# Step rows and input rows of a selective scan's unit, fetched by two transfers on two queues

## The chip, the cores and the metric

One Trainium2 chip, one of its cores. Its engines run their own instruction streams and meet at semaphores: PE (TensorE, with PEld for its weight loads), DVE (VectorE), ACT (ScalarE), POOL (GpSimd) and SP (SyncE, which here only issues transfers). An instruction that waits for a semaphore holds up everything behind it on its engine. 16 DMA engines carry out the transfers. The metric is device time of one launch in microseconds; lower is better.

## The reference

Two layers on x of (4 images, 16 x 16 pixels, 192 channels). The first is a gated state-space block: group norm, in-projection to 2 x 96 channels, a 3x3 depthwise convolution with silu, a selective scan in four directions, layer norm, gate, out-projection. The second is a linear attention (12 heads, 64 features) and then an attention in which 6 of the 12 heads are chosen for each image; both with layer norm and residual. The scan is the part that matters here:

```python
def step(h, inp):
    u_t, d_t, B_t, C_t = inp
    dA = jnp.exp(d_t[..., None] * As)
    h = h * dA + (d_t * u_t)[..., None] * B_t[:, :, None, :]
    y = jnp.einsum('bkcn,bkn->bkc', h, C_t)
    return (h, y)
```

with 96 channels, 16 states, 256 pixels, 4 directions and 4 images.

## The kernel before

Each engine's program is written out by hand. The work of the scan is cut into 96 units, numbered u. There are 8 scans (4 images x 2 pairs of directions), each of 12 units; a unit holds 16 channels x 8 states on the 128 partitions and 2 directions x 256 pixels along the row (512 elements). For a unit

- ScalarE makes the decay, exp(step x A), in two instructions (`expo`, L763),
- VectorE makes the drive, input x B (`drive_of`, L1055), and runs the scan itself (`scan`, L1066), in this order,
- GpSimd multiplies the states by C (`weigh`, L586),
- TensorE sums the 8 states of a channel, for three units at a time (`sum_states`, L1395 and L1401).

Decay and drive need the step sizes and the inputs (step x value) of 16 channels, each repeated on 8 partitions. For each scan these rows are made once, on 96 partitions (`step2`); the inputs' half is made by GpSimd (`pre_inp`, L575). SyncE writes them to DRAM (`keep_step`, L451, semaphore step_kept; two buffers in turn), and then reads them back for each unit with every row repeated 8 times (`repeat_step`, L463): one transfer of 512 KB, 128 rows of 4 KB, of which the first half is the steps and the second half the inputs. The tile `in_rep` has four slots; unit u + 4 goes where unit u was, so its transfer waits for decay u and drive u. The rows of C travel the same way, 256 KB at a time in rows of 2 KB (`repeat_c`, L444).

Between the units each engine does other steps of the two layers. Tables say after which unit: ACT_SIDE, DVE_SIDE, PE_SIDE, POOL_SIDE, SP_SIDE. "81: t1.0 gT.2 hT.1" in ScalarE's table means that after decay 81 it copies the turned probabilities of the odd heads of image 0 (three copies, L648), the gate of image 2 (L648) and the hidden state of image 1 (L838). TensorE's results go through four PSUM banks, `ring0` to `ring3`, in a fixed order: a bank is filled again only when the engine that reads it has said so (semaphores s_free0 to s_free3). A fixed number of filler matmuls (`fill_in`, L1235), whose results nobody reads, stands ahead of many of TensorE's steps.

The three loops around the change, in the units' order: SyncE does its side items of unit u and then fetches unit u + 4; ScalarE makes decay u and then its side items; VectorE makes drive u, scan u and then its side items.

Of the kernel before, what the change touches and what calls it, by code (L numbers as in the profile page):

```python
# [29 lines left out]
TOK = WAYS * L  # L30
# [3 lines left out]
SN = 8  # L34
GRP = P // SN
GROUPS = DI // GRP
PARTS = NS // SN
UNITS = PARTS * GROUPS
# [10 lines left out]
IN_SLOTS = 4  # L49
# [17 lines left out]
SLOT_COUNT = SCANS * UNITS  # L67
# [115 lines left out]
def hybrid_kernel(nc, x, in_proj_w, conv_w, conv_b, x_proj_w, dt_w, dt_b, A_logs, Ds, norm_g, norm_b, out_proj_w,  # L183
# [5 lines left out]
    with ExitStack() as ctx:  # L189
        ctx.enter_context(nc.allow_non_contiguous_dma(reason="small parameter vectors"))  # L190

        def sb(name, shape, dt=F32):
            return ctx.enter_context(nc.sbuf_tensor(name, shape, dt))
# [24 lines left out]
        def sem(name):  # L218
            return ctx.enter_context(nc.semaphore(name))


        step_rows = nc.dram_tensor("step_rows", [2, DI, 2 * TOK], F32, kind="Internal").ap()
# [7 lines left out]
        def bank(name):  # L230
            return banks[ring[name][1]]
# [58 lines left out]
        in_rep = sb("in_rep", [P, IN_SLOTS, 2, TOK])  # L290
# [57 lines left out]
        S["outd"] = [sem(f"s_outd{b}") for b in range(IMG)]  # L348
        S["x"] = [sem(f"s_x{n}") for n in range(IMAGES)]
        S["c_there"] = [sem(f"s_c_there{i}") for i in range(PARTS)]  # L350
        S["in_there"] = [sem(f"s_in_there{i}") for i in range(IN_SLOTS)]
        free = [sem(f"s_free{i}") for i in range(FINAL_RING)]
        pe_side, act_side, dve_side, pool_side, sp_side = (beside(s) for s in (PE_SIDE, ACT_SIDE, DVE_SIDE, POOL_SIDE, SP_SIDE))
# [5 lines left out]
        def reuse(eng, name):  # L359

            _, at, held = ring[name]
            if held:
                eng.wait_ge(free[at], held)
            elif at >= RING + PARTS + 1:
                eng.wait_ge(S["y_ev"], IMAGES)
            elif at >= RING:
                eng.wait_ge(S["state"], SLOT_COUNT)
# [23 lines left out]
        def unit(u):  # L391

            n, g = u // UNITS, u % UNITS
            third, q = g % GROUPS % CHUNKS, g % GROUPS // CHUNKS
            return n // PER_IMAGE, n % PER_IMAGE, g // GROUPS, PER_CHUNK * third + q
# [5 lines left out]
        def _(sp):  # L401
# [5 lines left out]
            for i in range(PARTS):  # L407
                rows = DIRS * GROUPS
# [25 lines left out]
            def keep_c(n):  # L434

                taken(sp, f"d{n}")
                sp.dma_start(c_rows[n % 2].rearrange("i s t -> (i s) t"), step2[DI:, 0, :]).then_inc(S["c_kept"], 16)

            def repeat_c(n, i):

                sp.wait_ge(S["c_kept"], 16 * (n + 1))
                if n:
                    sp.wait_ge(S["outp"], UNITS * (n - 1) + GROUPS * (i + 1))
                sp.dma_start(c_rep[:, i, :], c_rows[n % 2, i].unsqueeze(0).to_broadcast([GRP, SN, TOK])).then_inc(S["c_there"][i], 16)  # L444

            def keep_step(n):

                sp.wait_ge(S["step"], n + 1)
                if n >= 2:
                    sp.wait_ge(S["decay"], UNITS * (n - 1))  # L450
                sp.dma_start(step_rows[n % 2], step2[0:DI, :, :].rearrange("p a t -> p (a t)")).then_inc(S["step_kept"], 16)  # L451

            def repeat_step(u):

                _, _, _, g = unit(u)
                n = u // UNITS
                if u % UNITS == 0:
                    sp.wait_ge(S["step_kept"], 16 * (n + 1))
                if u >= IN_SLOTS:
                    sp.wait_ge(S["decay"], u - IN_SLOTS + 1)  # L460
                    sp.wait_ge(S["drive"], u - IN_SLOTS + 1)
                rows = step_rows[n % 2, GRP * g:GRP * (g + 1), :]
                sp.dma_start(in_rep[:, u % IN_SLOTS, :, :].rearrange("p a t -> p (a t)"),  # L463
                             rows.unsqueeze(1).to_broadcast([GRP, SN, 2 * TOK])).then_inc(S["in_there"][u % IN_SLOTS], 16)

            keep_c(0)
            keep_step(0)
            for u in range(2):
                repeat_step(u)
            for i in range(PARTS):  # L470
                repeat_c(0, i)
            for u in range(2, IN_SLOTS):
                repeat_step(u)
            def side(step, n):

                if step == "kc":
                    keep_c(n)
                elif step == "ks":
                    keep_step(n)
                else:  # L480
                    repeat_c(n, int(step[1]))

            for item in sp_side[0]:
                side(*item)
            for u in range(SLOT_COUNT):
                for item in sp_side[u + 1]:
                    side(*item)
                if u + IN_SLOTS < SLOT_COUNT:
                    repeat_step(u + IN_SLOTS)
# [9 lines left out]
        def _(pool):  # L499
# [78 lines left out]
            def weigh(u):  # L578

                _, _, part, c16 = unit(u)  # L580
                if u % GROUPS == 0:
                    pool.wait_ge(S["c_there"][part], 16 * (u // UNITS + 1))
                pool.wait_ge(S["state"], u + 1)
                if u >= SLOTS:
                    pool.wait_ge(S["y_mm"], u - SLOTS + 1)
                g.tensor_tensor(outp[:, u % SLOTS, :], state[:, u % STATE_SLOTS, :], c_rep[:, part, :],  # L586
                                ALU.mult).then_inc(S["outp"], 1)
# [53 lines left out]
        def _(act):  # L641
            a = nc.scalar

            def evac(name, *copies):

                fetched(act, name)
                for dst, src in copies:
                    ins = a.copy(dst, src)  # L648
                ins.then_inc(freed(name), 1)
# [103 lines left out]
            def expo(u):  # L753

                _, back, part, c16 = unit(u)
                slot = u % IN_SLOTS
                act.wait_ge(S["in_there"][slot], 16 * (u // IN_SLOTS + 1))
                if u >= DECAY_SLOTS:
                    act.wait_ge(S["state"], u - DECAY_SLOTS + 1)
                kept = slice(0, L - 1) if back else slice(1, L)  # L760
                for e in range(WAYS):
                    at = (part * DIRS + WAYS * back + e) * GROUPS + c16
                    ins = a.activation(decay[:, back, u % DECAY_SLOTS, e, kept],  # L763
                                       in_rep[:, slot, 0, :].rearrange("p (e l) -> p e l", e=WAYS)[:, e, kept],
                                       ACT.Exp, scale=a_neg[:, at:at + 1])
                ins.then_inc(S["decay"], 1)

            def turned_probs(n, j):

                if n:  # L770
                    act.wait_ge(S["weighed"], n)
                name = f"pt{n}{j}"
                evac(name, (probT[:, j % 2, j // 2, :], bank(name)[:, :]))
# [126 lines left out]
                side(*item)  # L900
            for u in range(SLOT_COUNT):
                expo(u)
                for item in act_side[u + 1]:
                    side(*item)
            for item in act_side[SLOT_COUNT + 1]:
# [4 lines left out]
        def _(dve):  # L910
# [135 lines left out]
            def drive_of(u):  # L1046

                _, _, part, c16 = unit(u)
                slot = u % IN_SLOTS
                if u % GROUPS == 0:  # L1050
                    dve.wait_ge(S["b_there"], PARTS * (u // UNITS) + part + 1)
                dve.wait_ge(S["in_there"][slot], 16 * (u // IN_SLOTS + 1))
                if u:
                    dve.wait_ge(S["state"], u)
                v.tensor_tensor(drv[:, :], in_rep[:, slot, 1, :], b_bc[part][:, :], ALU.mult).then_inc(S["drive"], 1)  # L1055
# [154 lines left out]
            for u in range(SLOT_COUNT):  # L1210
                drive_of(u)
                scan(u)
                for item in dve_side[u + 1]:
                    side(*item)
# [455 lines left out]
```

## Time and profile before

| | |
|---|---|
| runs (us) | 397.46, 397.60, 617.52; median 397.6 |
| the profiled execution | 396.75, of which the span of the core's instructions is 395.0 |
| mean granted TensorE clock | 0.988 of full |
| busy | PE 371.8 (94%), DVE 285.2 (72%), ACT 212.7 (54%), POOL 192.4 (49%) |
| moved by DMA | 61.85 MB, mean 157 GB/s over the span |
| in_rep transfers | 96 of 512 KB, median 6.5 us from issue to landing |

The run of 617.52 us stands apart from the other two. The units' scans start between 43 and 295 us of the span. Before that stand the norms, the weights and the first scan's rows; after it the end of the second layer for images 2 and 3. A busy PE counts fillers too.

### The profile page before, as it was taken

What the parts mean: (1) busy time and instruction counts of PE and PEld (TensorE: products, weight loads), DVE (VectorE), ACT (ScalarE), POOL (GpSimd) and SP (SyncE); (2) the same over time, 40 slices, a digit from 0 to 9 for tenths busy, and PEclk for the clock granted to TensorE, in tenths of its full rate; (3) what the DMA queues carried; (4) which work ended last, traced back from release to release, by engine and by line L of the source; (5) the groups of instructions that cost most, each with busy time, mean ns of one, the idle gap of its engine ahead of it and who ended that gap; (6) DMA issues with size and microseconds to landing.
All of it is one profiled execution on the core that took longest, in us unless ns stands there. A gap on an engine that the chain in (4) does not pass through costs nothing.

```text
span 395.0 us, 7870 instructions
## 1 busy us (share of the span) xinstructions
PE 371.8 (94%) x2805; PEld 288.6 (73%) x2805; DVE 285.2 (72%) x477; ACT 212.7 (54%) x553; POOL 192.4 (49%) x236
## 2 busy tenths in 40 slices
PE   7998969999999999999999999999999999999990
PEld 5878847787797775777767877767586668888770
DVE  4734887999689898999979989799793500553464
ACT  2576447567445574744855657836754431257530
POOL 5222673788187676579665725854362400210021
PEclk9999998999999999999999999999999999999996
DMA  5703999999979999988988996369910000000010
GB/s 115 138 19 100 239 263 254 255 284 262 232 176 256 243 241 264 248 212 223 252 189 222 248 240 171 92 189 253 246 49 1 2 0 2 0 22 2 1 42 20
DMA packets 26240, 61.85 MB, mean 157 GB/s; under 512 B 6935, under 2 KB 10969, under 8 KB 26201
## 3 DMA queue, kind: packets, MB, share of 16 engines
q1 hardware_dynamic: 26201, 61.35, 62.6%
q8 instruction: 22, 0.36, 0.4%
q14 instruction: 17, 0.14, 0.1%
HBM read 57.15 MB, written 4.19 MB: 155 GB/s over the span
## 4 chain that ended last, share of the span: by engine, by line
PE 77%; DVE 9%; DMA 5%; ACT 4%; issue 2%; POOL 1%; SPq 1%; POOLq 0%; ACTq 0%; DVEq 0%
PE ring L1235 15%; PE y_acc L1401 6%; PE ring L1524 5%; PE y_acc L1235 5%; PE ring L1518 5%; DMA in_rep<-step_rows 4%; DVE state L1066 3%; PE b_bc L1376 3%; PE y_acc L1395 3%; PE ring L1445 2%; PE ring L1469 2%; PE ring L1598 2%; PE ring L1535 2%; PE ring L1415 2%; PE ring L1428 2%
## 5 line engine op out<-in xcount | busy, mean ns | idle before, releaser
L586 POOL TENSOR_TENSOR outp<-state,c_rep 128x512 f32<-128x512 f32 x96 | 123.4, 1301 | 62.5 <-PE y_acc L1401 30.2
L1066 DVE TENSOR_TENSOR_SCAN state<-decay,drv 128x512 f32<-128x512 f32 x96 | 117.2, 1220 | 13.6 <-ACT decay L763 6.4
L763 ACT ACTIVATE decay<-in_rep,a_neg 128x255 f32<-128x255 f32 x192 | 86.1, 500 | 54.3 <-DMA in_rep<-step_rows 45.7
L1235 PEld LDWEIGHTS ring<-ident 128*128 128x128 f32 x726 | 90.8, 193 | 23.5 <-issue 15.9
L1235 PE MATMUL ring<-ident 128*128 128x128 f32 (+1 forms) x726 | 99.2, 281 | 4.1 <-ACT room_h L678 2.9
L1055 DVE TENSOR_TENSOR drv<-in_rep,b_bc 128x512 f32<-128x512 f32 x96 | 66.4, 692 | 10.7 <-PE b_bc L1376 2.0
L601 POOL TENSOR_SCALAR mv<-mv 128x2 f32<-128x2 f32 x16 | 4.6, 287 | 82.0 <-DVE mv L1080 81.5
L1401 PE MATMUL y_acc<-outp,band 128*32 128x256 f32 x192 | 33.8, 610 | 0.0
L1235 PE MATMUL y_acc<-ident 128*32 128x128 f32 (+1 forms) x236 | 30.9, 276 | 0.0
L1235 PEld LDWEIGHTS y_acc<-ident 128*32 128x32 f32 (+1 forms) x236 | 24.3, 118 | 5.5 <-issue 5.2
L1524 PE MATMUL ring<-kvw,tT 96*128 96x480 f32 (+1 forms) x52 | 22.9, 567 | 0.0
L1518 PE MATMUL ring<-tT,qw 96*128 96x256 f32 (+1 forms) x88 | 20.7, 380 | 0.8 <-ACT tT L648 0.8
L1395 PE MATMUL y_acc<-outp,band 128*32 128x256 f32 x192 | 20.2, 390 | 0.8 <-POOL outp L586 0.8
L1140 DVE TENSOR_REDUCE nmax<-ring 128x2 f32<-128x512 f32 x19 | 12.2, 683 | 11.3 <-PE ring L1415 7.7
L1518 PEld LDWEIGHTS ring<-tT,qw 96*128 96x128 f32 (+1 forms) x88 | 16.1, 189 | 3.9 <-ACT tT L648 1.0
L1376 PE MATMUL b_bc<-xs,w_b 96*128 96x256 f32 x64 | 16.5, 385 | 0.0
L784 ACT ACTIVATE prob<-ring,nmax 128x256 f32<-128x256 f32 x38 | 14.8, 481 | 2.4 <-DVE nmax L1140 2.4
L648 ACT COPY room_c<-ring 128x512 f32<-128x512 f32 (+1 forms) x20 | 10.9, 546 | 9.1 <-PE ring L1428 7.0
L1376 PEld LDWEIGHTS b_bc<-xs,w_b 96*128 96x128 f32 x64 | 11.6, 189 | 4.9 <-issue 2.5
L1524 PEld LDWEIGHTS ring<-kvw,tT 96*128 96x128 f32 (+1 forms) x52 | 9.2, 190 | 7.4 <-issue 7.3
L1173 DVE RECIPROCAL arec<-b_bc 128x24 f32<-128x24 f32 x1 | 0.3, 306 | 19.6 <-PE b_bc L1551 19.6
L1469 PE MATMUL ring<-room_c 96*96 96x256 f32 x54 | 13.1, 395 | 0.0
(339 smaller groups left out, 622.4 us busy)
## 6 DMA issues: line engine op xcount, KB each, us to landing
in_rep<-step_rows SPq DMA_DIRECT2D x96, 512.0 KB, 6.5
c_rep<-c_rows SPq DMA_DIRECT2D x16, 256.0 KB, 6.1
step_rows<-step SPq DMA_DIRECT2D x8, 384.0 KB, 4.8
x_tok<-in_x_dram SPq DMA_DIRECT2D x4, 192.0 KB, 3.7
out_dram<-res SPq DMA_DIRECT2D x4, 192.0 KB, 2.0
room_a<-in_L_attn_w_qkv_dram SPq DMA_DIRECT2D x1, 432.0 KB, 6.5
c_rows<-step SPq DMA_DIRECT2D x8, 32.0 KB, 6.4
room_h<-in_L_conv_in_proj_w_dram SPq DMA_DIRECT2D x1, 144.0 KB, 4.9
```

What stands on the lines that cost most here:

```text
L586: g.tensor_tensor(outp[:, u % SLOTS, :], state[:, u % STATE_SLOTS, :], c_rep[:, part, :], ALU.mult).then_inc(S["outp"], 1)
L763: ins = a.activation(decay[:, back, u % DECAY_SLOTS, e, kept], in_rep[:, slot, 0, :].rearrange("p (e l) -> p e l", e=WAYS)[:, e, kept], AC ...
L784: a.activation(prob[:, i, q, :], bank(name)[:, q * L:(q + 1) * L], ACT.Exp, bias=nmax[:, i, q:q + 1]).then_inc(S["prob"] if q == 0 else fr ...
L1055: v.tensor_tensor(drv[:, :], in_rep[:, slot, 1, :], b_bc[part][:, :], ALU.mult).then_inc(S["drive"], 1)
L1066: v.tensor_tensor_scan(state[:, u % STATE_SLOTS, :][:, order], held[:, order], drv[:, :][:, order], 0.0, ALU.mult, ALU.add).then_inc(S["st ...
L1235: t_.matmul(dst[:, 0:wide], ident[:, 0:cols], ident[:, 0:wide], start=True, stop=True)
L1376: ins = t_.matmul(b_bc[part][:, e * L:(e + 1) * L], w_b[:, k, part, :], xs[:, i, e, :], start=True, stop=True)
L1395: t_.matmul(y_acc[rows, 0:L], band[:, at:at + CHUNK], outp[:, u % SLOTS, 0:L], start=False, stop=False)
L1401: t_.matmul(y_acc[rows, 0:L], band[:, at:at + CHUNK], turned, start=False, stop=(g == PER_IMAGE * UNITS - BATCH)).then_inc(S["y_mm"], 1)
L1469: ins = t_.matmul(b_[0:DI, 0:L], taps[:, i, :], xpad[:, n, i // 3:i // 3 + SIDE, i % 3:i % 3 + SIDE], start=(i == 0), stop=(i == 8))
L1518: ins = t_.matmul(b_[:, u * L:(u + 1) * L], qw[0:CK + c, c, i * P:(i + 1) * P], tT[0:CK + c, c, at0:at0 + L], start=(c == 0), stop=(c == 1))
L1524: ins = t_.matmul(b_[:, 0:w], tT[0:CK + c, c, at:at + P], kvw[0:CK + c, c, j, :], start=(c == 0), stop=(c == 1))
```

## The change

A unit's rows come by two transfers of 256 KB, 128 rows of 2 KB each. SyncE fetches the steps, into the first half of the slot, once decay u is done; it no longer waits for drive u. ScalarE's own queue fetches the inputs, into the second half: after decay u it waits for drive u - 1 and issues the inputs of unit u + 3. The inputs have semaphores of their own (inp_there), for which the drive waits; the decay waits for in_there as before, now for the steps alone. For the first unit of a scan both transfers wait for step_kept, each on its own engine. The inputs of the first four units are fetched by SyncE. `keep_step` also waits for the drives of the scan before the last, since the buffer that it writes is now read by two transfers.

```diff
+        S["inp_there"] = [sem(f"s_inp_there{i}") for i in range(IN_SLOTS)]
...
                 if n >= 2:
                     sp.wait_ge(S["decay"], UNITS * (n - 1))
+                    sp.wait_ge(S["drive"], UNITS * (n - 1))
...
                 if u >= IN_SLOTS:
                     sp.wait_ge(S["decay"], u - IN_SLOTS + 1)
-                    sp.wait_ge(S["drive"], u - IN_SLOTS + 1)
-                rows = step_rows[n % 2, GRP * g:GRP * (g + 1), :]
-                sp.dma_start(in_rep[:, u % IN_SLOTS, :, :].rearrange("p a t -> p (a t)"),
-                             rows.unsqueeze(1).to_broadcast([GRP, SN, 2 * TOK])).then_inc(S["in_there"][u % IN_SLOTS], 16)
+                rows = step_rows[n % 2, GRP * g:GRP * (g + 1), 0:TOK]
+                sp.dma_start(in_rep[:, u % IN_SLOTS, 0, :],
+                             rows.unsqueeze(1).to_broadcast([GRP, SN, TOK])).then_inc(S["in_there"][u % IN_SLOTS], 16)
+
+            def repeat_first_inputs(u):
+
+                g = unit(u)[3]
+                rows = step_rows[0, GRP * g:GRP * (g + 1), TOK:]
+                sp.dma_start(in_rep[:, u, 1, :], rows.unsqueeze(1).to_broadcast([GRP, SN, TOK])).then_inc(S["inp_there"][u], 16)
 
             keep_c(0)
             keep_step(0)
             for u in range(2):
                 repeat_step(u)
+                repeat_first_inputs(u)
             for i in range(PARTS):
                 repeat_c(0, i)
             for u in range(2, IN_SLOTS):
                 repeat_step(u)
+                repeat_first_inputs(u)
...
+            def repeat_input(u):
+
+                g, n = unit(u)[3], u // UNITS
+                if u % UNITS == 0:
+                    act.wait_ge(S["step_kept"], 16 * (n + 1))
+                act.wait_ge(S["drive"], u - IN_SLOTS + 1)
+                rows = step_rows[n % 2, GRP * g:GRP * (g + 1), TOK:]
+                act.dma_start(in_rep[:, u % IN_SLOTS, 1, :],
+                              rows.unsqueeze(1).to_broadcast([GRP, SN, TOK])).then_inc(S["inp_there"][u % IN_SLOTS], 16)
...
             for u in range(SLOT_COUNT):
                 expo(u)
+                if u and u + IN_SLOTS - 1 < SLOT_COUNT:
+                    repeat_input(u + IN_SLOTS - 1)
                 for item in act_side[u + 1]:
                     side(*item)
...
-                dve.wait_ge(S["in_there"][slot], 16 * (u // IN_SLOTS + 1))
+                dve.wait_ge(S["inp_there"][slot], 16 * (u // IN_SLOTS + 1))
```

The change adds 21 lines, so lines of the new kernel have higher numbers (decay L772, ScalarE's new DMA L784). ScalarE's stream around decay 81 of the kernel before, with the semaphores that each row waits for (s_state: scans done; s_filled: TensorE's results; s_in_there: transfers landed):

```order
L763 ACTIVATE decay<-in_rep,a_neg 128x255 [waits s_state,s_in_there1]
L763 ACTIVATE decay<-in_rep,a_neg 128x255
L648 COPY room_c<-ring2 128x512 [waits s_filled]
L648 COPY room_c<-ring3 128x512 [waits s_filled]
L648 COPY room_c<-ring0 128x512 [waits s_filled]
L648 COPY gT<-ring2 96x256 [waits s_filled]
```

The same place with the change; the DMA fetches the inputs of unit 84, the first of the last scan:

```order
L772 ACTIVATE decay<-in_rep,a_neg 128x255 [waits s_state,s_in_there1]
L772 ACTIVATE decay<-in_rep,a_neg 128x255
L784 DMA in_rep<-step_rows 128x1x512 [waits s_drive,s_step_kept]
L657 COPY room_c<-ring2 128x512 [waits s_filled]
L657 COPY room_c<-ring3 128x512 [waits s_filled]
L657 COPY room_c<-ring0 128x512 [waits s_filled]
L657 COPY gT<-ring2 96x256 [waits s_filled]
```

Ahead of the copies now stands a DMA that waits for drive 80 and for the last scan's rows in DRAM. TensorE's stream at the same place is the same in both but for line numbers; before (room_f is the gate, prob the probabilities, s_free2 says that ring bank 2 has been read):

```order
L1428 MATMUL ring0<-ident,prob 128x128 [waits s_free0]
L1428 MATMUL ring0<-ident,prob 128x128 x3
L1235 MATMUL ring2<-ident 128x128 [waits s_free2]
L1503 MATMUL ring2<-ident,room_f 96x128 [waits s_gate]
L1503 MATMUL ring2<-ident,room_f 96x128
L1395 MATMUL y_acc<-outp,band 32x256 [waits s_outp]
L1395 MATMUL y_acc<-outp,band 32x256 x2
L1401 MATMUL y_acc<-outp,band 32x256 x3
L1508 MATMUL ring2<-outT,gT 128x192 [waits s_free2]
```

Nothing moved here; the filler into ring2 waits until ScalarE's first copy out of that bank, which is one of the copies above. SyncE's stream at the last scan, before:

```order
L463 DMA in_rep<-step_rows 128x1x1024 [waits s_drive,s_decay] x2
L451 DMA step_rows<-step 96x1024 [waits s_decay,s_step]
L444 DMA c_rep<-c_rows 128x1x512 [waits s_outp,s_c_kept]
L463 DMA in_rep<-step_rows 128x1x1024 [waits s_drive,s_decay,s_step_kept]
L463 DMA in_rep<-step_rows 128x1x1024 [waits s_drive,s_decay] x5
```

and with the change:

```order
L464 DMA in_rep<-step_rows 128x1x512 [waits s_decay] x2
L453 DMA step_rows<-step 96x1024 [waits s_drive,s_decay,s_step]
L445 DMA c_rep<-c_rows 128x1x512 [waits s_outp,s_c_kept]
L464 DMA in_rep<-step_rows 128x1x512 [waits s_decay,s_step_kept]
L464 DMA in_rep<-step_rows 128x1x512 [waits s_decay] x5
```

The order of SyncE's transfers stays; each waits for one semaphore less and carries half the bytes.

## Rows read from the trace of the kernel before

**Rows 1.** Page: busy us, share and count; then the last chain by engine.
```profile
PE 371.8 (94%) x2805; PEld 288.6 (73%) x2805; DVE 285.2 (72%) x477; ACT 212.7 (54%) x553; POOL 192.4 (49%) x236
...
PE 77%; DVE 9%; DMA 5%; ACT 4%; issue 2%; POOL 1%; SPq 1%; POOLq 0%; ACTq 0%; DVEq 0%
```

**Rows 2.** Windows: stretch, us, busy us (instructions) by engine, clock, DMA share, GB/s.
```profile
36.00:57.00 21.00, 17.89 (x118) 13.48 (x116) 16.55 (x22) 11.66 (x29) 12.29 (x12) 1.00 0.98 237
57.00:297.00 240.00, 236.50 (x1767) 178.37 (x1768) 210.93 (x286) 143.04 (x365) 152.91 (x151) 0.99 0.88 220
264.00:297.00 33.00, 33.00 (x223) 23.75 (x222) 29.00 (x34) 20.26 (x60) 16.29 (x13) 1.00 0.74 184
...
80.00:100.00 20.00, 20.00 (x158) 15.95 (x157) 18.73 (x22) 12.89 (x29) 17.20 (x15) 1.00 0.98 266
```

**Rows 3.** Waits: waiter <- awaited: us in total, times, longest us.
```profile
ACT decay L763 <- DMA in_rep<-step_rows: 45.7, 42, 2.6
...
DVE state L1066 <- ACT decay L763: 6.4, 11, 2.2
...
PE ring L1235 <- ACT room_h L678: 1.9, 1, 1.9
...
SPq L461 <- DVE drv L1055: 137.3, 78, 4.4
```

**Rows 4.** DMA issues (KB each, median us to landing); windows with and without C rows.
```profile
in_rep<-step_rows SPq DMA_DIRECT2D x96, 512.0 KB, 6.5
c_rep<-c_rows SPq DMA_DIRECT2D x16, 256.0 KB, 6.1
...
42.50:44.50 2.00, 2.00 (x12) 1.47 (x10) 1.97 (x3) 0.91 (x2) 1.26 (x1) 1.00 1.11 270
50.00:52.00 2.00, 0.42 (x4) 0.15 (x3) 1.70 (x3) 0.67 (x3) 1.86 (x3) 1.00 1.03 231
```

**Rows 5.** Tile in_rep: SyncE's issue, ns min/median/max.
```profile
L463 SPq DMA_DIRECT2D in_rep<-step_rows x96: 514/515/1587, 35.8 to 284.2; - x96
```

**Rows 6.** Timeline, ACT and then DVE, at 125 us: start, us, instruction [idle before].
```profile
125.50 0.91 ACT L763 ACTIVATE decay<-in_rep,a_neg 128x255 f32<-128x255 f32 x2 [1.14 <-DVE state L1066]
126.31 0.81 ACT L740 ACTIVATE step<-ring,dtb 96x256 f32<-96x256 f32 x2
...
125.50 0.70 DVE L1055 TENSOR_TENSOR drv<-in_rep,b_bc 128x512 f32<-128x512 f32 x1
```

**Rows 7.** Timeline, ACT from decay 81 on; then DVE's drive 79.
```profile
250.49 0.91 ACT L763 ACTIVATE decay<-in_rep,a_neg 128x255 f32<-128x255 f32 x2 [0.41 <-DVE state L1066]
251.80 0.59 ACT L648 COPY room_c<-ring 128x512 f32<-128x512 f32 x1 [0.41 <-PE ring L1428]
...
254.49 0.37 ACT L648 COPY gT<-ring 96x256 f32<-96x256 f32 x1
...
248.45 0.68 DVE L1055 TENSOR_TENSOR drv<-in_rep,b_bc 128x512 f32<-128x512 f32 x1
```

**Rows 8.** Timeline, POOL and SP: the last scan's inputs made, its rows written.
```profile
255.86 1.26 POOL L575 TENSOR_TENSOR step<-step,xs 96x512 f32<-96x512 f32 x1
...
257.14 0.31 SPq L451 DMA_DIRECT2D step_rows<-step  x1
```

**Rows 9.** Line 451 from 256 to 260 us: that write's landing.
```profile
DMA to landing us min/median/max: 3.4/3.4/3.4
```

**Rows 10.** Timeline, PE at the gate's transposes and out-projection; then DVE's residual.
```profile
253.81 0.39 PE L1235 MATMUL ring<-ident 128*128 128x128 f32 x2
...
255.77 0.92 PE L1508 MATMUL ring<-outT,gT 96*128 96x192 f32 x4
...
256.72 0.56 DVE L1098 TENSOR_TENSOR x_tok<-x_tok,ring 128x384 f32<-128x384 f32 x1 [2.22 <-PE ring L1508]
```

**Rows 11.** Window after the first gaps of PE (columns as in rows 2).
```profile
57.00:62.00 5.00, 4.65 (x20) 3.97 (x21) 2.89 (x4) 2.85 (x9) 1.91 (x2) 0.66 1.04 255
```

**Rows 12.** Windows of tile decay alone: DVE and ACT busy us (instructions), clock, DMA.
```profile
80.00:100.00 20.00, 10.95 (x9) 8.05 (x18) 1.00 0.98 266
```

## The prediction

> **What bounds the kernel now.** I read, in this order, the busy shares and the chain that ended last, the waits, the DMA issues, and then the timelines of the units where the change puts a new wait.
>
> The profiled execution took 396.75 us, its span 395.0; the median of the runs shown, 397.6, stands 0.85 above the execution that I sum against.
>
> TensorE is busy 94% and carries 77% of the last chain [rows 1]. Between 36 and 297 us, where the 96 units run, it idles only 21.00 - 17.89 = 3.1 us in the first stretch and 240.00 - 236.50 = 3.5 us in the rest; from 264 us to the end of the scan it never idles [rows 2]. Its instruction stream is fixed, and much of it is filler matmuls that run whether data are early or late. So an input that comes sooner can win back at most those 6.6 us, while one that comes late stops the stream and moves all that follows.
>
> The input transfers look like a bottleneck from ScalarE: it waits 45.7 us for them, 42 times, some 1.1 us each [rows 3]. But VectorE's scans wait only 6.4 us for the decays, and TensorE's longest wait for ScalarE in the scans is one of 1.9 us [rows 3]. SyncE spends 137.3 us waiting for VectorE's drive to release a slot [rows 3]: its queue is not short of issue time.
>
> **The change, part by part.**
>
> *The bytes.* A unit's 512 KB become 2 x 256 KB over the same 16 engines. In dense stretches these are already full: share 1.03 at 231 GB/s [rows 4]. The price of 2 KB rows in place of 4 KB rows can be read from the C rows, which are such transfers: the window in which the two of the first scan move shows 270 GB/s at a share of 1.11 [rows 4]. So I take no change of rate; the bounds are the two rates of these windows, 231 and 270. The Trainium skill's DMA: Bandwidth & Descriptors (Rules for kernel authors) wants 1 MiB or more in one DMA for full bandwidth, which speaks against halving; its fit of 2.0 us plus bytes/436 GB/s (Anatomy of one DMA, for the other issue path) would make an estimate of 3.2 us for the whole and 5.2 us for two halves one after the other. The trace shows instead that the fixed part is hidden, since a 512 KB transfer takes 6.5 us to land, a 256 KB one 6.1 [rows 4], and several are under way at once.
>
> *Earlier release of the step half.* It now waits for its decay alone, not for the drive about 2 us later. That can take most of ScalarE's 1.1 us off 42 units. What is late next is TensorE, so I count it as a buffer; its worth lies between 0 and the 6.6 us above.
>
> *Four more issues on SyncE at the start.* Each costs 0.515 us [rows 5], so 2.1 us, beside a transfer queue that is full by then. I take 0.
>
> *92 issues on ScalarE.* Each may cost between nothing (if it passes while the decays run) and 0.515 us [rows 5], together 0 to 47 us of an engine that is busy 143 of the 240 us [rows 2]. Each also waits for the previous unit's drive. Where inputs are in time, as at 125 us, a decay pair and a drive start together at 125.50; the pair ends at 126.41, the drive at 126.20, and the step behind the pair starts at 126.31 [rows 6]. With an issue after the drive it starts at 126.20 + 0.52 = 126.7, 0.4 later. Where ScalarE waited 1.1 us for a transfer, it starts earlier than now. TensorE waits for ScalarE in few places now, and a wait there would grow by up to 0.5. Bounds: the whole gain of 6.6 us, and 10 us of loss (20 of the 92 issues each holding TensorE for 0.5). I take +0.5 for this and the release together.
>
> *The wait for the next scan's rows, the main term.* The issue for a scan's first unit (u = 12n) also waits until that scan's step rows are written, and it stands three units ahead, behind decay 12n - 3. Until now that wait stood on SyncE alone, which has nothing else to do. On ScalarE every later step queues behind it. For most scans the rows are written in time, or the block is short and TensorE waits for nothing behind it. For the last scan they are not:
>
> - ScalarE runs decay 81 at 250.49 and goes on at 251.80 with the three copies of turned probabilities and at 254.49 with the gate's copy [rows 7]. (It gets there some 2 us later with the change: the issue before it, behind decay 80, waits for a drive that starts at 248.45 [rows 7].)
> - The last scan's inputs are made by GpSimd at 255.86, for 1.26 us; SyncE writes the rows at 257.14 [rows 8], and they land 3.4 us later [rows 9], at 260.54. GpSimd's order is set by work ahead of it that the change doesn't touch.
> - So ScalarE stands until 260.54, issues (0.52, to 261.06), and only then copies the first head: 261.06 + 0.59 = 261.65.
> - That copy frees ring bank 2. TensorE's next work in this bank is the filler at 253.81 [rows 10], which would start at about 261.75. TensorE moves by 261.75 - 253.81 = 7.9 us. Behind it ScalarE needs two more copies and the gate's, 2 x 0.59 + 0.37, to 263.2; TensorE reaches the output projection 255.77 - 253.81 = 1.96 later [rows 10], at 263.7, so that adds nothing.
> - VectorE's residual waits for that projection (2.22 us idle before it [rows 10]), and the next drive comes after the residual. So VectorE and GpSimd move along, and no idle TensorE is left before 297 to absorb it [rows 2].
>
> *The clock.* After the two gaps before 57.35 us, the granted clock averaged 0.66 over the five us from 57 to 62 [rows 11], at its lower level (1.2 GHz) for most of them: 5 x 0.34 = 1.7 us lost. A gap of nearly 8 us is longer than both, so I add 1.7; bounds 0 and twice that.
>
> **Sum:** 396.75 + 7.9 + 1.7 + 0.5 = 406.9, say 407 us.
>
> **The rivals.**
>
> *The block costs less than I think* (no change). Either the earlier step half wins back most of the 6.6 us, or ScalarE's queue isn't held as the order says. Then 396.75 + 7.9 + 1.7 - 6.6 = 399.8, or about 398 without the block. For it: ScalarE's 45.7 us of waits. Against: TensorE waits for ScalarE so little. It decides if TensorE's gaps before 250 us vanish. Chance 0.31, over 399 to 405.
>
> *ScalarE becomes the bound as well* (slower still). From 80 to 100 us it is busy 12.89 of 20 us [rows 2], with the decays of nine units (18 instructions) among it [rows 12]; nine issues would make it 17.5. If the issues can't overlap, it falls behind wherever several side steps stand together, and every copy that TensorE needs is late by several issues: the 10 us above instead of 0.5, so 416. For it: the busy share. Against: an average unit takes 240/89 = 2.7 us, against 0.9 for the decays, 0.5 for the issue and 0.7 for the rest (143 less 89 x 0.9, over the 89 units that this stretch holds). Chance 0.13, over 411 to 418.
>
> *Two queues fill the transfer engines better* (faster). If all 6.6 us of TensorE's idle time in the scans and the 1.7 us of low clock went, and the block were hidden, 396.75 - 8.3 = 388.5. It would need ScalarE to pass decay 81 without standing. Against: the engines are full already [rows 4], and fillers don't shorten. Chance 0.03.
>
> *Half rows move more slowly* (slower). At 231 instead of 250 GB/s a 512 KB unit takes 2.3 us, not 2.1. In the some 60 units in which transfers set the pace of ScalarE that would be 10 us, part of it covered by fillers: 411 to 417. Against: the C rows. Chance 0.03.
>
> **Numbers.** My forecast, 405 to 411 with 407 likeliest, has 0.50. The measurement tells about 2% from no change, 8 us here, so the border is 405.55. Slower: the forecast but for its lowest part (0.47), the second and the fourth rival: 0.63. Within 2%: 0.34. Faster: 0.03. The range from 400 to 415 leaves out the fast rival, the lowest part of the first and the top of the second.
>
> **What would show it.** In the changed kernel's trace: ScalarE idle from about 253 to 260.5 us (plus what earlier shifts add) behind the decays of unit 81, with its DMA issue at the end; TensorE idle some 8 us up to the filler of the gate's transposes, put down to ScalarE's copy; the clock low for a few us after; TensorE's gaps elsewhere about as now; ScalarE's waits for in_rep well below 45.7 us; the transfer rate in dense stretches unchanged. The prediction is wrong if ScalarE passes unit 81 without that stop, if TensorE finds other work meanwhile, or if TensorE's gaps before 250 us change by more than 3 us in sum.

## The result and the profile after

The changed kernel takes 408.76 us (median of four runs, 406.42 to 412.94), the kernel before 399.52 (397.46, 397.60, 401.44 and the 617.52 that stands apart). The ratio is 1.0229, 95% interval [1.0121, 1.0338]: slower, though the interval leaves open whether by more than 2%. Forecast were 407, 400 to 415. The profiled execution took 409.1 us, its span 407.4. In some runs of most kernels here, the one before included, TensorE's mean clock is lower and the time longer, and the ratios leave the most disturbed of them out.

The page after, as in [rows 1], and between its lines the granted clock in 40 slices of the span, in tenths:

```profile
PE 376.8 (92%) x2805; PEld 292.5 (72%) x2805; DVE 285.3 (70%) x477; ACT 213.0 (52%) x553; POOL 192.0 (47%) x236
...
PEclk9999999999999999999999999599968999999997
...
PE 49%; DVE 9%; issue 4%; POOL 3%; ACT 2%; DMA 1%; ACTq 1%; POOLq 0%; DVEq 0%
```

The work is the same, but the clock has a 5 in slice 26, around 260 us (a slice is 10.2 us), and a second dent (6 and 8) in slices 30 and 31.

ScalarE's timeline after, at the place of [rows 7] (start, us, instruction [idle before]):

```profile
249.16 0.95 ACT L772 ACTIVATE decay<-in_rep,a_neg 128x255 f32<-128x255 f32 x2
257.80 0.53 ACTq L784 DMA_DIRECT2D in_rep<-step_rows  x1
258.37 1.56 ACT L657 COPY room_c<-ring 128x512 f32<-128x512 f32 x3 [8.26 <-DMA step_rows<-step]
260.26 0.37 ACT L657 COPY gT<-ring 96x256 f32<-96x256 f32 x1 [0.33 <-PE ring L1524]
```

GpSimd's and SyncE's, as in [rows 8]:

```profile
253.03 1.26 POOL L584 TENSOR_TENSOR step<-step,xs 96x512 f32<-96x512 f32 x1
...
254.32 0.31 SPq L453 DMA_DIRECT2D step_rows<-step  x1
```

And TensorE's, as in [rows 10]:

```profile
250.91 0.60 PE L1449 MATMUL ring<-ident,prob 128*128 128x128 f32 x4
259.01 0.80 PE L1256 MATMUL ring<-ident 128*128 128x128 f32 x2 [7.50 <-ACT room_c L657]
259.59 0.64 PE L1524 MATMUL ring<-ident,room_f 128*96 128x128 f32 x2
...
262.02 1.65 PE L1529 MATMUL ring<-outT,gT 96*128 96x192 f32 x4
```

Decay 81 ends at 250.1. The rows are written at 254.32 and land 3.5 us later; then ScalarE issues, at 257.80, and only then copies. TensorE stands from 251.51 to 259.01.

The waits after, as in [rows 3]:

```profile
SPq L464 <- ACT decay L772: 135.5, 71, 7.4
...
ACT decay L772 <- DVE state L1087: 25.4, 28, 2.4
...
DVE x_tok L1119 <- PE ring L1529: 12.3, 1, 12.3
...
DVE state L1087 <- ACT decay L772: 5.6, 6, 2.3
...
ACT decay L772 <- DMA in_rep<-step_rows: 2.7, 4, 1.1
...
PE ring L1256 <- ACT prob L803: 1.7, 2, 1.4
```

SyncE still waits as long for slots (135.5 us, before 137.3), now for the decays alone. ScalarE's wait for in_rep fell from 45.7 to 2.7 us, and VectorE's for the decays hardly moved (6.4, now 5.6): the 43 us bought VectorE almost nothing. The residual waits 12.3 us for TensorE, and the drives behind it come late.

Windows after (columns as in [rows 2]); the first four stand against [rows 2, 4, 11], the fifth ends where TensorE stops, the last three lie at the two low stretches of the clock:

```profile
36.00:57.00 21.00, 19.43 (x129) 14.94 (x128) 17.83 (x23) 13.39 (x33) 12.86 (x12) 1.00 0.98 288
42.50:44.50 2.00, 2.00 (x10) 1.46 (x9) 1.86 (x3) 0.03 (x1) 1.27 (x1) 1.00 1.06 293
50.00:52.00 2.00, 0.81 (x5) 0.40 (x8) 1.82 (x3) 0.91 (x2) 2.00 (x2) 1.00 1.06 315
57.00:62.00 5.00, 5.00 (x28) 3.91 (x27) 4.59 (x6) 3.48 (x9) 3.42 (x3) 1.00 1.04 331
...
57.00:251.50 194.50, 190.10 (x1432) 145.26 (x1430) 173.72 (x232) 114.98 (x283) 129.08 (x129) 1.00 0.82 229
254.50:259.00 4.50, 0.00 (x0) 0.00 (x0) 0.00 (x0) 0.63 (x2) 0.00 (x0) 0.51 0.48 146
259.00:264.80 5.80, 5.79 (x28) 4.14 (x28) 1.06 (x3) 3.62 (x11) 0.00 (x0) 0.50 0.82 243
298.90:309.20 10.30, 10.30 (x55) 8.20 (x50) 4.88 (x9) 3.36 (x9) 2.53 (x2) 0.50 0.01 2
```

Two things here were not forecast. The same engines, as full as before, carry 288 GB/s in place of 237 in the first 21 us, and 315 in place of 231 at 50 us; TensorE idles 1.6 us in the first 21 us, not 3.1, and the low clock of [rows 11] is gone in this execution. The unit scans run some 4 us early from unit 9 (61.94 us, before 66.16) to unit 78 (241.11, before 244.94). Then, from 298.9 us on, the clock is at its lower level (1.2 GHz) for 10.3 us in which TensorE never stands: 10.3 x 0.50 = 5.1 us lost, on top of 5.8 x 0.50 = 2.9 us behind the stand.

The DMA issues, as in [rows 4]:

```profile
in_rep<-step_rows SPq DMA_DIRECT2D x100, 256.0 KB, 5.1
in_rep<-step_rows ACTq DMA_DIRECT2D x92, 256.0 KB, 5.0
c_rep<-c_rows SPq DMA_DIRECT2D x16, 256.0 KB, 5.3
```

A half lands 5.0 or 5.1 us after its issue, where the whole took 6.5.

### The profile page after: what moved, and what is told of

Same layout as the page of the kernel before. It is cut to its first block, busy times and chain, and to the rows that moved or that the text cites. A ratio compares the mean times of both kernels' runs of the same rounds, so it can differ in the third digit from the quotient of the medians.

```text
span 407.4 us, 7888 instructions
## 1 busy us (share of the span) xinstructions
PE 376.8 (92%) x2805; PEld 292.5 (72%) x2805; DVE 285.3 (70%) x477; ACT 213.0 (52%) x553; POOL 192.0 (47%) x236
## 4 chain that ended last, share of the span: by engine, by line
PE 49%; DVE 9%; issue 4%; POOL 3%; ACT 2%; DMA 1%; ACTq 1%; POOLq 0%; DVEq 0%
PE ring L1256 6%; DVE state L1087 4%; PE ring L1545 4%; PE ring L1539 4%; PE y_acc L1422 3%; PE y_acc L1256 2%; DVE drv L1076 2%; PE ring L1466 2%; POOL outp L595 2%; PE ring L1619 2%; PE ring L1556 2%; PE ring L1572 2%; PE y_acc L1416 2%; PE ring L1436 2%; PE ring L1449 1%
## 5 line engine op out<-in xcount | busy, mean ns | idle before, releaser
L1087 DVE TENSOR_TENSOR_SCAN state<-decay,drv 128x512 f32<-128x512 f32 x96 | 117.2, 1221 | 12.4 <-ACT decay L772 5.6
L1256 PEld LDWEIGHTS ring<-ident 128*128 128x128 f32 x726 | 90.9, 193 | 30.4 <-issue 15.9
L1256 PE MATMUL ring<-ident 128*128 128x128 f32 (+1 forms) x726 | 99.4, 281 | 10.8 <-ACT room_c L657 7.5
L772 ACT ACTIVATE decay<-in_rep,a_neg 128x255 f32<-128x255 f32 x192 | 85.5, 502 | 31.2 <-DVE state L1087 25.4
L1422 PE MATMUL y_acc<-outp,band 128*32 128x256 f32 x192 | 33.9, 612 | 0.0
L1256 PE MATMUL y_acc<-ident 128*32 128x128 f32 (+1 forms) x236 | 30.9, 276 | 0.0
L1256 PEld LDWEIGHTS y_acc<-ident 128*32 128x32 f32 (+1 forms) x236 | 24.3, 118 | 5.5 <-issue 5.2
L1416 PE MATMUL y_acc<-outp,band 128*32 128x256 f32 x192 | 21.1, 406 | 0.6 <-POOL outp L595 0.6
L803 ACT ACTIVATE prob<-ring,nmax 128x256 f32<-128x256 f32 x38 | 14.8, 481 | 5.0 <-DVE nmax L1161 2.9
L543 POOL TENSOR_TENSOR rs<-mv,neg_half 128x2 f32<-128x2 f32 x16 | 11.8, 738 | 1.3
```

The costliest lines, as they stand in the source:

```text
L803: a.activation(prob[:, i, q, :], bank(name)[:, q * L:(q + 1) * L], ACT.Exp, bias=nmax[:, i, q:q + 1]).then_inc(S["prob"] if q == 0 else fr ...
L1087: v.tensor_tensor_scan(state[:, u % STATE_SLOTS, :][:, order], held[:, order], drv[:, :][:, order], 0.0, ALU.mult, ALU.add).then_inc(S["st ...
L1256: t_.matmul(dst[:, 0:wide], ident[:, 0:cols], ident[:, 0:wide], start=True, stop=True)
L1416: t_.matmul(y_acc[rows, 0:L], band[:, at:at + CHUNK], outp[:, u % SLOTS, 0:L], start=False, stop=False)
L1422: t_.matmul(y_acc[rows, 0:L], band[:, at:at + CHUNK], turned, start=False, stop=(g == PER_IMAGE * UNITS - BATCH)).then_inc(S["y_mm"], 1)
```

## The experiments

Theory A: the loss is ScalarE's stand for the last scan's rows and the clock behind it. Rival B: the 92 issues make ScalarE late everywhere. Open besides: where the 4 us of gain come from, and what the second low stretch is. Kernels of one batch of four share their runs of the kernel before, whose medians were 397.25, 397.25 and 397.06 us (kernels 1 to 4, 5 to 8, 9 to 12). A ratio is to these runs.

**1. The last scan's first inputs issued by SyncE** (changed kernel; ScalarE skips unit 84 and waits for the rows at unit 85, behind decay 82):

```diff
+                if u + IN_SLOTS == SLOT_COUNT - UNITS:
+                    sp.wait_ge(S["drive"], u + 1)
+                    sp.dma_start(in_rep[:, u % IN_SLOTS, 1, :], ...)
...
```

> The changed kernel, but for the one input transfer of unit 84, which SyncE issues behind that unit's step half; ScalarE keeps the other 91 issues and no longer waits for the last scan's rows behind decay 81. Theory A (the time went into ScalarE's stand at unit 81 and the low clock behind it): the 7.5 us gap of TensorE before the gate's filler goes, and the low stretch after it, so 408.8 - 7.5 - 2.9 = 398, and as TensorE ran some 4 us ahead of the kernel before up to unit 78, down to 395. Rival B (ScalarE's issues make it late everywhere): the gap goes, but other waits for ScalarE grow in its place, 403 or more.

Measured: 399.96 us (396.05 to 404.28), ratio 0.9994 [0.995, 1.0038]. The median lies between the two forecasts, and the seven runs that the ratio counts, 396.05 to 401.58, lie mostly in theory A's. The stand before the gate is gone, but it moved one unit on. ScalarE's timeline in this kernel, and where TensorE waits behind it:

```profile
255.38 0.91 ACT L777 ACTIVATE decay<-in_rep,a_neg 128x255 f32<-128x255 f32 x2
260.15 0.53 ACTq L789 DMA_DIRECT2D in_rep<-step_rows  x1
261.05 0.51 ACT L777 ACTIVATE decay<-in_rep,a_neg 128x255 f32<-128x255 f32 x1 [4.77 <-DMA step_rows<-step]
...
263.13 0.64 PE L1481 MATMUL ring<-ident,room_h 128*96 128x128 f32 x4 [1.83 <-ACT room_h L845]
```

Behind decay 82 it waits 4.77 us for the same rows, now with decay 83 queued first, and TensorE stands 1.83 us for a step behind that. Most of the loss went with the copies out of the queue: for A, but not a clean undoing.

**2. The wait alone, miscounted** (kernel before):

```diff
+                if u + 3 == SLOT_COUNT - UNITS:
+                    act.wait_ge(S["step_kept"], 16 * IMAGES)
```

> The kernel before, whole 512 KB transfers all issued by SyncE, with one wait added: ScalarE waits behind decay 81 until the last scan's step rows have landed. Theory A: TensorE stands some 7.5 to 8 us before the gate's filler and works at the lower clock for some us after it, so 8 to 12 us slower than before, 407 to 411. Rival B (the stand costs that much only because ScalarE also has 92 issues): 402 or less. Rival C (the slowdown comes from halves): the same as before.

Measured: 397.62 us, 1.0012 [0.9978, 1.0046]. There are eight scans, not four: the count was reached long before, ScalarE never waited, and none of the theories was tested. The run shows how well an equal kernel repeats: within 0.5%.

**3. Halves with the changed kernel's releases, all issued by SyncE:**

```diff
-                if u and u + IN_SLOTS - 1 < SLOT_COUNT:
-                    repeat_input(u + IN_SLOTS - 1)     # ScalarE
+                if u and u + IN_SLOTS - 1 < SLOT_COUNT:
+                    repeat_input(u + IN_SLOTS - 1)     # SyncE, ahead of repeat_step(u + IN_SLOTS)
```

> All transfers in halves with their own semaphores and releases as in the changed kernel, but SyncE issues the input halves too, in ScalarE's order (unit u+3's inputs ahead of unit u+4's steps); ScalarE issues none and waits for no rows. Theory A: no stand at unit 81, time 394 to 398, within 2 us of the kernel in which only unit 84's transfer is SyncE's. Rival B (92 issues on ScalarE cost): at least 5 us faster than that kernel. Rival C (half transfers are slower): 403 or more.

**4. Halves alone, both behind decay and drive:**

```diff
+                    sp.wait_ge(S["drive"], u - IN_SLOTS + 1)    # in repeat_step
...
+                    repeat_input(u + IN_SLOTS)                  # SyncE, right behind repeat_step(u + IN_SLOTS)
```

> Halving alone: two transfers of 256 KB in place of each of 512 KB, both issued by SyncE, both behind decay and drive as before, the first units' too. Theory A1 (the 4 us gained up to unit 78 come from the first transfers of the program, which land earlier in halves, and the gap and low clock at 55 to 62 us that go with them): 394 to 397, as with lagging halves. Theory A2 (they come from the earlier release of the step half): the same as before, within 1.5 us. Rival C (half transfers are slower): 403 or more.

Measured: 393.60 us, 0.9912 [0.9883, 0.9942], for the third; 393.46, 0.9894 [0.9858, 0.9929], for the fourth. Both beat both kernels, the one before by 1%, and they are equal: the changed kernel's releases, which let go of the steps earlier and of the inputs later, are together worth nothing, and the halves are worth 3.8 us. The third is faster than the first kernel by 3.3 us by the ratios and 6.4 by the medians, where theory A said within 2 and rival B at least 5: the first still has a stand and ScalarE's issues. In the fourth kernel, the windows at the start of the first scan (before: 17.89 us busy at 237 GB/s, and a clock of 0.66 [rows 2, 11]):

```profile
36.00:57.00 21.00, 19.42 (x131) 15.23 (x130) 17.54 (x23) 13.79 (x35) 12.87 (x12) 1.00 0.95 282
...
57.00:62.00 5.00, 5.00 (x27) 3.90 (x26) 4.62 (x6) 3.09 (x8) 3.08 (x3) 1.00 0.99 282
```

TensorE idles 1.5 us less there and loses no 1.7 us to the clock. The unit scans tell the same: 3.9 us ahead of the kernel before at unit 9, 3.7 at unit 95. In halves a decay also waits for its steps alone, which land first; but unit 9's later half has landed at 59.74 us, its whole transfer before at 64.33, so the bytes themselves come sooner. The queue's row of the page (packets, MB, share of 16 engines' span), of before and then of halves alone:

```profile
q1 hardware_dynamic: 26201, 61.35, 62.6%
```

```profile
q1 hardware_dynamic: 40025, 61.36, 54.1%
```

The same bytes took 0.626 x 395.0 = 247 us of the 16 engines before and 0.541 x 391.2 = 212 now, 14% less.

**5. The wait alone, with the eighth scan's count** (kernel before):

```diff
+                if u + 3 == SLOT_COUNT - UNITS:
+                    act.wait_ge(S["step_kept"], 16 * SCANS)
```

> The kernel before with one wait added, now with the count of the eighth scan's rows: behind decay 81 ScalarE waits until they have landed; transfers whole and all SyncE's. Theory A (the stand is the cause by itself): TensorE stands 7 to 8 us before the gate's filler, the clock is low for some 10 us behind it, 404 to 412, against 397.25 for the kernel before. Rival B (it costs only together with ScalarE's own issues): 400 or less.

Measured: 405.55 us, 1.0209 [1.0155, 1.0263], 8.3 us more, in theory A's range. ScalarE's timeline and TensorE's in this kernel:

```profile
250.69 0.91 ACT L763 ACTIVATE decay<-in_rep,a_neg 128x255 f32<-128x255 f32 x2 [0.41 <-DVE state L1068]
260.73 1.56 ACT L648 COPY room_c<-ring 128x512 f32<-128x512 f32 x3 [9.14 <-DMA step_rows<-step]
...
261.37 0.79 PE L1237 MATMUL ring<-ident 128*128 128x128 f32 x2 [7.20 <-ACT room_c L648]
```

One wait, without a byte or an issue changed, gives the stand, its place and its price. Theory A holds for it.

**6. No missing rows for ScalarE** (changed kernel; units 84 to 86 by SyncE):

```diff
+                first = u + IN_SLOTS - 1 - (SLOT_COUNT - UNITS)
+                if 0 <= first < 3:
+                    sp.wait_ge(S["drive"], u)
+                    sp.dma_start(in_rep[:, (u - 1) % IN_SLOTS, 1, :], ...)
```

> The changed kernel, but SyncE issues the inputs of the last scan's first three units (84 to 86), each one unit behind its steps; ScalarE keeps 89 issues and meets no missing rows. Theory A (its stand for the rows is the whole loss): 393 to 396, within 2 us of the 393.6 of the kernel whose halves are all SyncE's; no stand behind decay 82, no low clock at 264 us. Rival B (the 92 issues cost by themselves): 397 or more.

Measured: 396.96 us (394.55 to 401.28), 0.9974 [0.9944, 1.0004]; its span is 393.1, that of the third kernel 391.9. The median lies at the border of the two forecasts. The issues cost 1.2 us in these two executions, 3.4 by the medians, which also hold a low clock that this kernel's runs show more often (0.974 to 0.98 in four of twelve, while the third has 0.981 in one of eleven and above 0.99 in the others). So where no rows are missing, rival B is right in kind and small in size. Where it shows most, ScalarE in this kernel and then in the third:

```profile
236.76 0.52 ACTq L790 DMA_DIRECT2D in_rep<-step_rows  x1
237.33 2.29 ACT L809 ACTIVATE prob<-ring,nmax 128x256 f32<-128x256 f32 x6 [2.11 <-DVE drv L1082]
```

```profile
234.72 2.28 ACT L803 ACTIVATE prob<-ring,nmax 128x256 f32<-128x256 f32 x6
```

Behind decay 78 the issue waits for a late drive, and the exponentials of the scores wait 2.11 us with it, of which TensorE feels 1.4 (the 1.7 us of the changed kernel's waits, PE ring L1256 <- ACT prob L803, holds it).

**7. Only the first four units halved** (kernel before; the diff shows this edit), and **10. only those whole** (the fourth kernel, with the first four transfers as before):

```diff
+                if u < IN_SLOTS:
+                    for a in range(2):
+                        rows = step_rows[0, GRP * g:GRP * (g + 1), a * TOK:(a + 1) * TOK]
+                        sp.dma_start(in_rep[:, u, a, :], ...).then_inc(S[("in_there", "inp_there")[a]][u], 16)
...
```

> The kernel before with only the first four units' transfers halved, each half with its own semaphore; units 4 to 95 whole as before. Theory A1 (the 3.8 us that halves gain lie in the start of the first scan, where TensorE stands and its clock falls): 393.5 to 395.5. Theory A2 (they need halves in the units behind it too, since a 512 KB transfer in 4 KB rows takes the engines longer): 396 to 398.

> Halves alone by SyncE, except that the first four units' transfers are whole, as before. If the gain of halves is all in the first four: 396.5 to 398. If the units behind them carry most of it: 393.5 to 395. With the first four alone having given 1.3 us of 3.8, the parts would leave 2.5 here: 394.7.

Measured: 395.96 us, 0.9942 [0.9906, 0.9979], and 395.27 us, 0.9977 [0.9935, 1.0019]. Each half of the edit gives a part (1.3 and 1.8 us by the medians), neither the whole, and both medians lie between the forecasts. The intervals overlap, and the tenth's holds 1, so the shares are not settled. In the traces the gain at unit 9 is 0.7 us for the seventh and 2.1 for the tenth, of the 3.9 above: it lies in the start of the first scan, but not in its four first transfers alone.

**8. Halved by partitions** (kernel before; two transfers of 64 rows of 4 KB):

```diff
+                for h in range(2):
+                    at = GRP * g + GRP // 2 * h
+                    rows = step_rows[n % 2, at:at + GRP // 2, :]
+                    sp.dma_start(in_rep[P // 2 * h:P // 2 * (h + 1), ...], ...)
...
```

> Each unit's 512 KB in two transfers of 256 KB as in the kernel of halves alone, but cut by partitions: 64 rows of 4 KB each, steps and inputs together; both behind decay and drive, one semaphore for both. If the gain of halves alone (393.5) comes from more transfers of a smaller size: 393 to 395. If it comes from 2 KB in place of 4 KB rows, or from the steps' landing ahead of the inputs: as before, 396 to 398.5, and the dense stretch at 43 to 57 us at 255 GB/s as before in place of 307.

Measured: 455.99 us, 1.1448 [1.1386, 1.151]; neither expectation. Windows of the fourth kernel and then of this one, whose profiled execution took 467.38 us, at the same place:

```profile
43.00:57.00 14.00, 12.43 (x88) 9.68 (x87) 13.21 (x15) 8.69 (x23) 10.50 (x10) 1.00 1.05 307
```

```profile
43.00:57.00 14.00, 8.08 (x55) 6.66 (x53) 7.16 (x9) 5.13 (x12) 6.77 (x7) 0.93 0.56 160
```

The engines are busy 0.56 in place of 1.05 while everything waits for them. The cut also halved the outermost count of the source, 16 channels to 8. The Trainium skill's DMA: Bandwidth & Descriptors (Why a DMA increments its semaphore by 16 and not by 1) says that a transfer is spread over as many engines, up to 16, as divide the outermost sizes of both sides: 8 here. The share of 0.56 agrees. So this run doesn't tell row length from number of transfers; that stays open.

**9. The changed kernel again:**

> The changed kernel once more, unaltered, beside the three others: its sum by parts so far is 393.5 (halves alone) + 8.3 (the wait alone) + 1.3 (ScalarE's issues) = 403.1, and 408.8 was measured. Theory A (the 5 us that are left are a second stretch of low clock at about 299 us): runs between 403 without it and 409 with it, with a granted clock of 0.98 and 0.967. Rival B (the parts don't add): about 408.8 whatever the clock.

Measured: 410.16 us (404.19 to 412.55), 1.0263 [1.0179, 1.0348]. One run took 404.19 at a mean clock of 0.983, two took 409.38 and 409.67 at 0.968 and 0.967, three 410.65 to 412.55 at 0.959 to 0.963: the 5 us go with the clock, as theory A has it. The profiled execution has the second low stretch too, and so has that of the first kernel, here in this order:

```profile
301.80:312.10 10.30, 10.30 (x53) 8.09 (x53) 5.19 (x9) 3.65 (x10) 2.80 (x3) 0.50 0.01 2
```

```profile
295.00:305.30 10.30, 10.30 (x51) 8.76 (x49) 4.64 (x8) 2.87 (x8) 2.34 (x2) 0.50 0.01 2
```

**11. Seven more fillers, at image 2's context** (changed kernel):

```diff
-    "kv01.2": 1, "sum.81": 2,
+    "kv01.2": 1, "cx.2": 4, "at.2": 3, "sum.81": 2,
```

> The changed kernel with seven more filler matmuls, four ahead of image 2's context (24 matmuls of 34 columns, which end where the second low stretch begins in the changed kernel's trace) and three ahead of the matmuls behind it; the 8 us stand stays. Seven by 0.28 us cost at most 2.0 us. Theory A (sparse matmuls there let the clock fall): the stretch at 299 us goes, 403 to 406, below the unaltered one. Rival B (the clock falls whatever stands there): 409 to 411.

Measured: 406.94 us, all six runs between 405.05 and 408.88, 1.0243 [1.0191, 1.0295]: above theory A's range and below B's. It is 3.2 us below the ninth by the medians, but the ratios, 1.0243 and 1.0263, can't be told apart. The mean clocks differ more clearly: 0.975 to 0.986 in these six runs, and in the ten of the changed kernel once 0.983 and nine times 0.959 to 0.976. In the changed kernel TensorE did this ahead of the fall at 298.9 us:

```profile
294.96 0.96 PE L1552 MATMUL ring<-v,eps_all 128*128 128x204 f32 x4
295.75 2.76 PE L1556 MATMUL ring<-v,room_a 128*128 128x34 f32 x24
298.45 1.67 PE L1436 MATMUL ring<-fk,fq 32*128 32x256 f32 x12
```

With the fillers around that work, the window of the same place:

```profile
296.00:307.00 11.00, 11.00 (x96) 9.51 (x95) 8.24 (x12) 4.34 (x12) 6.04 (x5) 1.00 0.01 1
```

The clock stays at its upper level (2.4 GHz); that more work is also faster is not shown. That a busy TensorE with such small matmuls comes ahead of the fall is shown, in three traces, and that the clock stays up in the one trace with work added there. But the kernel before runs the same 24 matmuls, at 288.18 us, with the clock at its upper level throughout [rows 2, 264 to 297 us], so they do not bring the fall by themselves. Why it comes in some executions and not in others stays open.

**12. Halves by SyncE and the wait** (the fourth kernel with the fifth's edit):

> Halves alone by SyncE, plus ScalarE's wait for the last scan's rows behind decay 81: the changed kernel without its 92 issues on ScalarE. If halves and wait add: 393.5 + 8.3 = 401.8, up to 407 with a second low stretch. If the issues on ScalarE carry the rest of the changed kernel's loss: 400 to 403 and no second low stretch.

Measured: 401.86 us, 1.0148 [1.0085, 1.021]. The sum 393.5 + 8.3 = 401.8 holds: halves and stand add. Five of the six runs lie between 401.69 and 404.06, one at 407.69 with a clock of 0.968. The second forecast, that ScalarE's issues carry the rest of the changed kernel's loss, names the same times and fits as well: the ninth kernel differs from this one by those issues and by the releases, which the third and fourth show to be worth nothing, and took 8.3 us more by the medians (1.0263 against 1.0148 by the ratios), at a clock of 0.968 or less in five of its six runs. So beside a stand the issues seem to cost more than in the sixth kernel, and the clocks point to the second low stretch coming oftener; but the intervals of the ratios overlap, and how the issues would bring it on is not shown.

## Why the prediction was right

The time came from the forecast's mechanism, and by luck from two further terms of opposite sign: the halves' gain, 3.8 us, and the second low stretch, 5.1.

- *The wait for the next scan's rows* (7.9 us) *and the clock behind it* (1.7): right in place and cause. TensorE stood 7.5 us and lost 2.9 to the clock behind it; the wait alone costs 8.3 us in the kernel before, 8.4 with halves, against 9.6 forecast. By the traces, unit 82's scan comes later behind unit 81's than in the kernel before by 8.9 us in the fifth kernel, 9.2 in the twelfth and 10.1 in the changed one.
- *The bytes* (no change of rate): wrong. This is the step that failed. Halves move the same bytes in 14% less engine time, worth 3.8 us. The price was read from a window in which C rows of 2 KB moved among 4 KB rows [rows 4], and such a mix hid what halves alone do: it showed 270 GB/s against 231, which was taken for the bounds of no change, and the fourth kernel reached 307 over 14 us. The Trainium skill's rule that one DMA should hold 1 MiB or more for full bandwidth (DMA: Bandwidth & Descriptors, Rules for kernel authors) would have had halves slower: here 256 KB transfers reach 288 GB/s where 512 KB ones reached 237.
- *Earlier release of the step half* (a buffer, between 0 and 6.6 us): 0 together with the inputs' later release, as the third and fourth kernels are equal.
- *92 issues on ScalarE* (+0.5 with the release; 0.527 us each, near the 0.515 of [rows 5]): too low; 1.2 us in the traces without missing rows, most of it at unit 78, and 3.4 by the medians. The second rival's 10 us of late copies did not come: ScalarE has slack, as its decays still wait 25.4 us for VectorE's scans. What the issues add by the clock is in the next term.
- *Not in the sum:* the second low stretch, 5.1 us. The traces have it only in kernels with ScalarE's issues (the changed one twice, and the first), no rival foresaw it, and its cause is open.

Together: 397.1 - 3.8 + 8.4 + 1.2 = 402.9 us without the second stretch and 408.0 with it; measured were 404.19 at the clock of 0.983, and 406.42 to 412.94 in the other nine runs. The profiled execution tells it directly, by its scans against those of the kernel before: 3.8 us ahead at unit 78, 3.1 at unit 81, 7.0 behind at unit 82, 12.4 at the end of the span. So 0.7 us went between units 78 and 81, where that issue stands, 10.1 with the stand and the clock behind it, and 5.4 after that, where the second stretch lies. The fast rival was given too little: that the engines are busy all the time does not say how many bytes they move in it. But what it promised is limited as the prediction said: the gain stops at unit 9, and behind that TensorE waits about as much as before (4.4 us up to the stand, before 3.5).

Of the signs named ahead, the stand of ScalarE and TensorE, the fall in ScalarE's waits and TensorE's gaps came (6.6 us before the gate, now 1.6 + 4.4 = 6.0); the unchanged transfer rate did not.

## What to carry to other kernels

When an issue with a wait moves from an idle engine to a busy one, look up in every round what stands behind it there; one wait of seven cost 8.3 us by itself, and the issues alone 1.2 to 3.4. Splitting a transfer may be worth doing without the second queue: halves by SyncE alone, 393.5 us, are the fastest version here. Read a rate from a window in which nothing but the transfers in question moves.

## What was not expected of the hardware

- Transfers of 256 KB in rows of 2 KB used the 16 engines better than 512 KB in rows of 4 KB: 212 us of their time for 61.36 MB, against 247. Whether the rows' length or the number of transfers does it is open. One queue does as well as two (from 43 to 57 us 307 GB/s with SyncE alone, 312 in the changed kernel, both at a share of 1.05).
- Cutting by partitions instead left them half idle (0.56) and cost 14%.
- TensorE's clock fell to its lower level for 10.3 us while TensorE was busy without a gap, behind 24 matmuls of 34 columns; the kernel before runs these at the upper level, and one run of the changed kernel, 404.19 us, has a mean clock of 0.983.
